# Opening second-order attention inside the second experts' tail: weights, one batch's scales and two tiles made ahead

## The reference

```
logits = einsum('bsh,eh->bse', x, Wg)               # 8 experts, each takes its 128 best tokens of a batch
h1 = gelu(einsum('bekh,ehf->bekf', ex, W1) + b1)     # F = 1024
out = G * (einsum('bekf,efh->bekh', h1, W2) + b2)    # added back to the rows it came from
...
q, k, v = x @ Wq, x @ Wk, x @ Wv                     # 16 heads of 32
S_K = g * S_K + k k';  C_prev = g * C_QV;  G = g * G + k (k' C_prev);  C_QV = C_prev + q v'
o = q' (S_K C_QV - G);   y = o @ Wo                  # g = 0.99, step by step over the tokens
```

## Time and profile before

| what | us |
|---|---|
| median of 3 timed runs | 3533.43 |
| lowest, highest | 3532.81, 3549.98 |
| the profiled execution | 3529.74 |
| its span, first to last instruction | 3527.8 |
| PE busy in it | 3262.7 (92%) |
| DVE, ACT, POOL busy | 2266.3, 2043.5, 1375.0 |

### The profile page before, as it was taken

One profiled execution on the slowest core, in us unless ns is written; L12 is line 12 of the kernel. 1 busy time (PEld: TensorE's weight loads), 2 busy tenths in 40 slices (PEclk: granted clock), 3 DMA queues, 4 the chain that ended last, 5 costly groups with the idle time before them and its releaser, 6 DMA issues. The chain is left out here.

```text
span 3527.8 us, 137586 instructions
## 1 busy us (share of the span) xinstructions
PE 3262.7 (92%) x55606; PEld 2885.2 (82%) x55606; DVE 2266.3 (64%) x6633; ACT 2043.5 (58%) x6370; POOL 1375.0 (39%) x2094
## 2 busy tenths in 40 slices
PE   8938999789965999989999999999998999999998
PEld 7938999777745999978888888888887888888877
DVE  6574555678866555546655555545555788888887
ACT  5555565555535565444444444434443699999996
POOL 5755565300004665423333333333333633333325
PEclk9979999999986999999999999999999999999999
DMA  4144343611134443420000000000001133333333
GB/s 131 49 146 104 89 96 66 169 32 49 56 107 159 95 93 84 105 60 4 4 4 4 4 4 4 4 4 3 4 4 35 31 120 118 118 107 102 104 99 101
DMA packets 202923, 235.34 MB, mean 67 GB/s; under 512 B 17968, under 2 KB 182976, under 8 KB 202304
## 3 DMA queue, kind: packets, MB, share of 16 engines
q1 hardware_dynamic: 177728, 192.99, 17.4%
q0 software_dynamic: 24576, 33.57, 5.6%
HBM read 147.46 MB, written 79.04 MB: 64 GB/s over the span
## 5 line engine op out<-in xcount | busy, mean ns | idle before, releaser
L2518 ACT ACTIVATE wa_S<-wa_S,wa_top 128x192 f32<-128x192 f32 x1024 | 462.7, 475 | 36.6 <-DVE wa_top L2614 36.6
L2057 POOL TENSOR_TENSOR so_OT<-so_O,so_OT 128x128 fp32r<-128x128 f32 x256 | 117.5, 459 | 745.5 <-ACT so_OT L1889 745.5
L1974 DVE TENSOR_TENSOR so_raw<-so_rows,so_masks 128x1024 f32<-128x1024 f32 x256 | 313.4, 1224 | 105.8 <-PE so_rows L1662 98.6
L1968 DVE COPY so_O<-so_bankX 128x128 f32<-128x128 f32 x256 | 74.6, 291 | 416.9 <-PE so_bankX L1775 347.3
L2614 DVE CUSTOM_DVE_ANT_0 wa_S<-wa_bank,wa_band 128x192 f32<-128x192 f32 x1024 | 294.9, 348 | 3.5 <-issue 3.4
L1897 ACT ACTIVATE so_KW<-so_bankU 128x128 f32<-128x128 f32 x256 | 71.2, 278 | 321.1 <-PE so_bankU L1669 321.1
L650 POOL DMA_INDIRECT sum_dram<-y,rows x128 | 223.6, 1747 | 29.4 <-issue 27.2
L2406 PE MATMUL wa_bank<-ident,wa_S 128*128 128x128 f32 x1536 | 221.2, 277 | 7.7 <-ACT wa_probT L2525 4.7
L2518 ACT ACTIVATION_READ_ACCUMULATOR wa_S<-wa_S,wa_top 128x1 f32 x1024 | 222.5, 217 | 0.0
L1691 PE MATMUL so_bankJ<-so_xnT,so_w 128*128 128x256 f32 x1500 | 210.2, 290 | 7.5 <-DVE so_xnT L1948 7.2
L728 ACT ACTIVATE m2e_hT<-m_bank,m2e_bias 128x256 fp32r<-128x256 f32 x256 | 126.9, 496 | 150.2 <-PE m_bank L680 144.2
(11 more groups left out here) (459 smaller groups left out, 9730.9 us busy)
## 6 DMA issues: line engine op xcount, KB each, us to landing
m_w_raw<-in_L_ffn_W_dram SPq DMA_DIRECT2D x64, 512.0 KB, 3.8
wa_V<-wa_V_dram SPq DMA_DIRECT2D x256, 128.0 KB, 3.0
sum_dram<-X SPq DMA_DIRECT2D x16, 1024.0 KB, 4.7
X<-sum_dram SPq DMA_DIRECT2D x16, 1024.0 KB, 8.3
wa_V_dram<-wa_V_new SPq DMA_DIRECT2D x32, 512.0 KB, 3.8
wa_V_rest<-wa_V_dram SPq DMA_DIRECT2D x128, 128.0 KB, 3.3
X<-in_L_attn_a_x_dram SPq DMA_DIRECT2D x8, 1024.0 KB, 11.7
xn_dram<-m2r_xn SPq DMA_DIRECT2D x16, 512.0 KB, 4.5
```

The costliest lines, as they stand in the source:

```text
L1968: nc.vector.tensor_copy(O[:, t % UT], bX[:, O_AT]).then_inc(s_["O_copied"], 1)
L1974: nc.vector.tensor_tensor(AB[:, t % 2].rearrange("p h m t -> p h (m t)"), rows4[:, :, 0:2 * P], masks[:].rearrange("p m t -> p (m t)")[:, ...
L2057: nc.gpsimd.tensor_tensor(OT[:, 1, t % (2 * UT)], O[:, t % UT], OT[:, 0, t % (2 * UT)].bitcast(F32), ALU.subtract).then_inc(s_["O_ready"], 1)
L2518: nc.scalar.activation(S[:, n % 2, z], S[:, n % 2, z], ACT.Exp, bias=top[:, n % 2, z:z + 1], scale=-1.0, accum_out=sums[:, i % 2, SET * c ...
```

## The change

- `w_raw` and the even half of the split weights (`w_even`) are allocated outside the experts' stage and live on. The new class `SecondOrderOpening` lays second-order attention's raw weights into `w_raw` and their high and low parts into `w_even`. The loop's AB and PT go on using the raw weights' place.
- SP: after the last low half of the experts' weights (`w_ready` = 32) it issues the seven weight loads, ahead of the reads of X.
- ACT: after its last gelu, and once expert 6 is through (`down_done` = 28), it casts the four weights, makes the root of batch 0's variances and, instead of POOL, the first two tiles, which go to the place of `R.L`.
- DVE: statistics of batch 0 (8 tiles) ahead of the b2 addition of pair 30; behind its weighing the variances, scales and the low halves of Wq, Wk, Wv, ahead of the b2 addition of pair 31. The statistics of batches 1 to 3 move into steps 2 to 13 of the loop, two a step, their variances into step 14, their scales into step 16.
- PE: the 30 warming products go; the turn of the first tiles stands ahead of the wait for the experts' end. Banks are ordered anew, so that J isn't one that the experts' last product uses.
- SP's masks wait for the last product only (`joined.products`); ACT waits for nothing of `joined`; DVE waits after its low halves.

```diff
--- before.py
+++ after.py
...
+    kept = ExitStack()
+    w_raw = kept.enter_context(nc.sbuf_tensor(f"{tag}_w_raw", [P, QUARTERS, F], F32))
+    w_even = kept.enter_context(nc.sbuf_tensor(f"{tag}_w_even", [P, 2, QUARTERS, F], F32R))
+    if opening:
+        opening.place(kept, w_raw, w_even)
...
+                if opening:
+                    sp.wait_ge(w_ready, PAIRS)
+                    opening.load(sp)
...
+                if opening:
+                    act.wait_ge(down_done, PAIRS - PE_)
+                    opening.cast(act)
+                    opening.root(act)
+                    opening.normalize(act)
...
+                def open_statistics(t, s):
+                    if isinstance(t, int) and t == PAIRS - 1:
+                        dve.wait_ge(R.row_back[0], 16 * (before + 1))
+                        opening.statistics(dve)
+
+                def open_scales(t, s):
+                    if isinstance(t, int) and t == PAIRS - 1:
+                        opening.scales_and_weights(dve)
...
+                if opening:
+                    skewed(dve, PAIRS, [(3, split_xT), (4, split_h), (4, open_statistics), (5, add_b2), (5, weigh), (4, open_scales), (0, split_w)],
+                           unroll=U)
+                else:
+                    skewed(dve, PAIRS, [(3, split_xT), (4, split_h), (5, add_b2), (5, weigh), (0, split_w), (7, stats)], unroll=U)
...
+            joined.products = (down_done, PAIRS)
...
+    def load(self, sp):
+        for n, name in enumerate("qkv"):
+            sp.dma_start(self.w_raw[:, n], self.A[f"L1_attn_a_W{name}"].rearrange("(c p) d -> p c d", p=P)).then_inc(self.sems[f"{name}_loaded"], 16)
+        wo_rows = self.A["L1_attn_a_Wo"].rearrange("(u p) d -> p u d", p=P)
+        for h in range(4):
+            to, of = ((h + 2) % 4 * 32, h * 32)
+            sp.dma_start(self.wo_raw[to:to + 32], wo_rows[of:of + 32]).then_inc(self.sems["o_loaded"], 16)
+
+    def cast(self, act):
+        for n, name in enumerate("qkv"):
+            act.wait_ge(self.sems[f"{name}_loaded"], 16)
+            self.nc.scalar.copy(self.w[:, 0, n], self.w_raw[:, n]).then_inc(self.sems["w_high"], 1)
+        act.wait_ge(self.sems["o_loaded"], 4 * 16)
+        self.nc.scalar.copy(self.wo[:, 0], self.wo_raw).then_inc(self.sems["w_high"], 1)
+
+    def root(self, act):
+        std_of_var(self.nc, act, self.R, self.sems["var_ready"], self.sems["std_ready"], self.FIRST)
+
+    def normalize(self, act):
+        act.wait_ge(self.sems["scaled"], 1)
+        for j in range(2):
+            self.nc.scalar.activation(self.rows[:, j], self.R.X[:, j, :], ACT.Identity, scale=self.R.rstd[:, j:j + 1], bias=self.R.shift[:, j:j + 1]
+                                      ).then_inc(self.sems["rows_ready"], 1)
+
+    def statistics(self, dve):
+        self.chain = Chain(dve, self.sems["step"])
+        for i in range(TB):
+            last = self.nc.vector.bn_stats(self.R.raw[:, i, :], self.R.X[:, i, :])
+        self.chain.then(last)
+
+    def scales_and_weights(self, dve):
+        variances(self.nc, self.chain, self.R, self.sems["var_ready"], self.FIRST)
+        self.low_weights(dve, 0)
+        dve.wait_ge(self.sems["std_ready"], 1)
+        scales(self.nc, self.chain, self.R, self.FIRST)
+        self.nc.vector.memset(self.R.turnstile[:], 0.0).then_inc(self.sems["scaled"], 1)
+        self.low_weights(dve, 1)
+        self.low_weights(dve, 2)
+
+    def low_weights(self, dve, n):
+        dve.wait_ge(self.sems["w_high"], n + 1)
+        self.nc.vector.tensor_tensor(self.w[:, 1, n], self.w_raw[:, n], self.w[:, 0, n].bitcast(F32), ALU.subtract).then_inc(self.sems["w_ready"], 1)
...
-                joined.wait_left(sp)
...
+                sp.wait_ge(*joined.products)
...
-                joined.wait_left(pe)
...
-                for _ in range(30):
-                    nc.tensor.matmul(bC[:, 0:P], R.ident[:], R.ident[:], start=True, stop=True)
                 turn_x(0)
+                joined.wait_left(pe)
...
-                joined.wait_left(act)
-                std_of_var(nc, act, R, s_["var_ready"], s_["std_ready"], FIRST)
...
+                    if t == NEXT_DONE + 1:
+                        std_of_var(nc, act, R, s_["var_ready"], s_["std_ready"], NEXT, 2)
...
-                c = layernorm_scales(nc, dve, R, s_["step"], s_["var_ready"], s_["std_ready"], FIRST)
-                nc.vector.memset(R.turnstile[:], 0.0).then_inc(s_["scaled"], 1)
...
+                joined.wait_left(dve)
...
+                    if NEXT_AT <= t < NEXT_DONE:
+                        for early in range(TB + 2 * (t - NEXT_AT), TB + 2 * (t - NEXT_AT) + 2):
+                            dve.wait_ge(R.row_back[early // TB], 32)
+                            ins = nc.vector.bn_stats(R.raw[:, early, :], R.X[:, early, :])
+                        if t == NEXT_DONE - 1:
+                            c.then(ins)
+                    if t == NEXT_DONE:
+                        variances(nc, c, R, s_["var_ready"], NEXT)
+                    if t == NEXT_DONE + 2:
+                        dve.wait_ge(s_["std_ready"], 2)
+                        scales(nc, c, R, NEXT)
+                        nc.vector.memset(R.turnstile[:], 0.0).then_inc(s_["scaled"], 1)
...
-                normalize(0)
-                normalize(1)
                 pool.wait_ge(s_["w_ready"], 4)
+                pool.wait_ge(s_["QT_ready"], 1)
...
```

More of the change, by code:

```diff
@@ L301, in _, with top_k_experts @@
                     nc.gpsimd.tensor_tensor(R.X[:, i, :], R.X[:, i, :], th[:, i % 4], ALU.add).then_inc(x_ready, 1)
-def top_k_experts(nc, R, tag, A, C, before, with_weights=False):
+def top_k_experts(nc, R, tag, A, C, before, with_weights=False, opening=None):
     E, F, K = 8, 1024, 128
@@ L679, in up @@
                         for n, (c, a, b) in enumerate(steps):
-                            last = nc.tensor.matmul(bank[:, 0:2 * P], w_parts[:, par, a, c, f * P:(f + 1) * P], exT[:, s % 2, b, c],
+                            last = nc.tensor.matmul(bank[:, 0:2 * P], w_parts[par][:, a, c, f * P:(f + 1) * P], exT[:, s % 2, b, c],
                                                     start=(n == 0), stop=(n == len(steps) - 1))
@@ L1541, in _, with __init__, place @@
                     ins.then_inc(XK_ready, 1)
-def second_order_attention(nc, R, A, C, joined):
+class SecondOrderOpening:
+    FIRST = slice(0, TB)
+    def __init__(self, nc, R, A):
+        self.nc, self.R, self.A = nc, R, A
+        self.stage = Stage(nc, "so")
+        names = "step var_ready std_ready scaled rows_ready q_loaded k_loaded v_loaded o_loaded w_high w_ready".split()
+        self.sems = {n: self.stage.sem(n) for n in names}
+        self.rows = R.L[:].rearrange("p i e -> p (i e)").rearrange("p (j d) -> p j d", j=2)
+    def place(self, kept, w_raw, w_even):
+        self.kept = kept
+        raw = w_raw[:].rearrange("p q f -> p (q f)")
+        parts = w_even[:].rearrange("p a q f -> p (a q f)")
+        dense = 3 * HC * 2 * HID
+        self.raw = raw[:, 0:dense]
+        self.w_raw = self.raw.rearrange("p (n c d) -> p n c d", n=3, c=HC)
+        self.wo_raw = raw[:, dense:].rearrange("p (u d) -> p u d", d=HID)
+        self.w = parts[:, 0:2 * dense].rearrange("p (a n c d) -> p a n c d", a=2, n=3, c=HC)
+        self.wo = parts[:, 2 * dense:].rearrange("p (a u d) -> p a u d", a=2, d=HID)
+    def load(self, sp):
[34 more added lines that the diff above has]
+        self.nc.vector.tensor_tensor(self.w[:, 1, n], self.w_raw[:, n], self.w[:, 0, n].bitcast(F32), ALU.subtract).then_inc(self.sems["w_ready"], 1)
@@ L1573, in second_order_attention @@
         rows4 = ps("rows", (P, HG, 512))
-        bU, bC, bX, bJ = (ps(f"bank{n}") for n in "UCXJ")
-        names = """loaded step var_ready std_ready scaled xn_ready xT_done xT_ready QT_done QT_ready KT_done KT_ready V_done V_ready
-                   q_loaded k_loaded v_loaded o_loaded w_high w_ready xT_high O_copied O_high
+        bU, bJ, bC, bX = (ps(f"bank{n}") for n in "UJCX")
+        names = """loaded xn_ready xT_done xT_ready QT_done QT_ready KT_done KT_ready V_done V_ready xT_high O_copied O_high
                    QTg_ready KTg_ready row_done AB_ready PT_ready turned K_ready KQe_ready U_done U_ready Ug_ready C_done WT_ready
@@ L1629, in _ @@
             def _(sp):
-                joined.wait_left(sp)
-                for n, name in enumerate("qkv"):
-                    sp.dma_start(w_raw[:, n], A[f"L1_attn_a_W{name}"].rearrange("(c p) d -> p c d", p=P)).then_inc(s_[f"{name}_loaded"], 16)
-                wo_rows = A["L1_attn_a_Wo"].rearrange("(u p) d -> p u d", p=P)
-                for h in range(HG):
-                    sp.dma_start(wo_raw[crossed_rows(h)], wo_rows[head_rows(h)]).then_inc(s_["o_loaded"], 16)
+                sp.wait_ge(*joined.products)
                 for to, name in ((masks[:, 0], "upper"), (masks[:, 1], "lower"), (decay_t[:], "decay_t"), (to_end[:], "to_end")):
@@ L1678, in turn_x @@
                 def turn_x(p):
```

(17 more changed lines are left out.)

57 lines of the change are left out of this document (26 added, 31 removed).

## The result

The changed kernel takes 3560.02 us (median of 11 runs, 3554.01 to 3567.18), the one before 3540.14 (11 runs beside it, 3529.29 to 3552.80): 1.0053 times as long, 95% interval 1.0037 to 1.0069. The forecast was 3518, with a range of 3513 to 3526 and 0.05 for slower. It is outside the range, on the side of a slower kernel.

The account below looks back on a forecast made before the run. At the seam a chain through DVE, ACT, POOL and the weight loads was taken as the bound, in the loop PE. Terms -17.8 + 0.8 + 1.5 = -15.5 us gave 3514.2 profiled, 3518 as median, range 3513 to 3526.

Parts of the forecast that it names:

- The seam: Between the last expert product and the loop's first rows: rows at 1502.3 instead of 1520.12, gain 17.8 us.
- The b2 addition: DVE's addition for the last pair at the seam: 0.9 us late at most, 0.4 with overlap, taken as 0.8.
- the rule's price: At the seam: if idle PE fell to 1.2 GHz, first projections at half speed, gain 1.3 us smaller; not taken.
- The gather: Experts' second gather before PE's turn of a pair, sharing queues with the early loads: 0.8 us lost, bounds 0 and 6.3.
- The statistics in the loop: Statistics of batches 1 to 3 in steps 2 to 13: 0.6 us lost in step 2, 0.3 in step 3, others hidden.
- The loop. Together 1.5 us lost: The 256-step loop: DVE's moved statistics, variances and scales cost 0.6, 0.3, 0.5 and 0.1 us in steps 2, 3, 14, 16.
- forecast sum: Whole kernel: -17.8 (seam) + 0.8 (gather) + 1.5 (loop) = -15.5 us.
- The slower one: Rival, chance 0.05: without warming products PE's clock falls in the seam's gap and stays down into the first steps, 3539 us.
- Loads hold the gather: Rival, chance 0.10: on the experts' path the early weight loads cost 6.3 us instead of 0.8; gain 10, 3523.5 us.

Follow-up runs that it names:

- e11: The kernel before with 53 filler groups of small PE products, laid to keep block borders off the exposed places of the loop's steps: 3524.62 us, ratio 0.9965.
- e9: The changed kernel with 44 filler groups of small PE products in 23 steps, to keep block borders off the exposed places: 3512.83 us, 0.9936 of the kernel before.
- e5: The changed kernel with 701 filler wait instructions on PE over 26 steps, to keep block borders off the exposed places: 3568.04 us, 1.0097 of the kernel before.
- e12: e10 with the weight loads one pair later still, behind the turn of the last pair (31): 3509.26 us, 0.9899 of the kernel before.
- e7: e5 with second-order attention's weight loads issued later, behind the turn of pair 30: 3565.11 us, 1.0091 of the kernel before.
- e10: e9 with the weight loads issued behind the turn of pair 30, as in e7: 3510.34 us, 0.9927 of the kernel before.
- e4: The changed kernel with 16 one-column PE products (64 instructions) added ahead of the first projection: 3528.69 us, 0.9981 of the kernel before.
- e1: The changed kernel with 30 one-column PE products (120 instructions) added ahead of the first projection: 3541.94 us, 1.0011 of the kernel before.

## Why the prediction was wrong, step by step

**The seam: right.** 17.8 forecast; 18.5 in the profile of the changed kernel, 18.0 between e11 and e9 (27.7 and 9.7 us from the last product's start to the first rows). The b2 addition was 0.8 us less late than taken. The clock stayed at 1.00, as the earlier trace rows had it; in e5 and e12, with the same gap, it didn't, and the first rows came 1.5 us later, about the 1.3 that the prediction gave as the rule's price. So that this term came out at the smaller price is in part luck.

**The gather: right mechanism, too small.** 0.8 forecast, bounds nothing and 6.3. The changed kernel:

```profile
1448.32 1.11 PE L672 MATMUL m_bank<-ident,m4e_ex_in 128*128 128x128 f32 x4 [2.94 <-DMA m4e_ex_in<-xn_dram,rows]
1449.08 6.88 PE L687 MATMUL m_bank<-m4e_exT,m_w_odd 128*128 128x256 f32 x48
```

The second gather goes out at 1442.20, and the turn of its rows starts 6.1 us later instead of 3.0 as in the earlier trace rows. The prediction took the queues as emptying 7 to 9 us after the first load had gone out (1436.33 here). Here they are still full from 1444 to 1446, 8 to 10 us behind it, and the DMA share (the last number but one) falls only then:

```profile
1444.00:1446.00 2.00, 1.38 (x12) 1.18 (x10) 0.58 (x2) 0.00 (x0) 0.00 (x0) 1.00 1.18 276
1446.00:1448.00 2.00, 0.00 (x0) 0.00 (x0) 0.70 (x3) 0.00 (x0) 1.07 (x2) 0.98 0.35 98
```

The stall is 2.94 us, and a second price was not in the sum at all: after it PE ran at half clock.

```profile
1448.30:1450.00 1.70, 1.68 (x8) 1.69 (x9) 0.53 (x1) 0.00 (x0) 1.40 (x2) 0.50 0.45 40
```

The turn took 1.11 instead of 0.60 and the following group 1 us more. Over the stretch it is 4.6 us. e7, e10 and e12 show it to be the loads: later by one pair 1.0 us is left, by two nothing.

**The statistics in the loop: right.** Steps 2, 3 and 14 grew by 0.64, 0.44 and 0.51 us (forecast 0.6, 0.3, 0.5), steps 4 to 13 by less than 0.1. The mask of P in step 2, against the earlier trace rows:

```profile
1509.09 1.23 DVE L2049 TENSOR_TENSOR m_w_raw<-so_rows,so_masks 128x1024 f32<-128x1024 f32 x1 [0.30 <-PE so_rows L1747]
...
1510.89 0.67 DVE L2057 TENSOR_TENSOR m_w_raw<-so_rows,so_masks 128x512 f32<-128x512 f32 x1
1513.40 1.22 DVE L2049 TENSOR_TENSOR m_w_raw<-so_rows,so_masks 128x1024 f32<-128x1024 f32 x1
```

**The step that failed: "The loop. Together 1.5 us lost".** It counted what the change adds to the loop's steps and took the rest of the 256 as unchanged, because no instruction in them changed. The 30 removed products were costed as time and as warmth, not as 120 places in PE's stream. That moved the borders: 51 stalls instead of 12, 45.8 us instead of 10.2. This term of +35.6 turned a gain into a loss. The whole loop lost 42.7, of which 1.6 are the statistics. The rest is there because steps with a stall grow by more than its gap: the steps 45 to 62, 136 to 157 and 235 to 253 of the changed kernel take 53.0 us more than in the kernel before, for 45.8 us of gaps. Why they do wasn't tested. The stalls of the kernel before were to be seen in its trace, as idle time by "issue" in rows that wait for nothing.

**Without it the sum holds.** e9 against e11: gather +4.7, seam -18.0, loop from the first rows to the last mask 1184.8 against 1183.1, +1.8: -11.5. The medians differ by 11.8. The forecast sum was -15.5, and the 4 us between are the gather's 4.7 where 0.8 stood.

**The rivals.** The slower one had the right sign, but its mechanism, a clock that stays down into the first steps, did not happen: the first group of projections ran at full clock. "Loads hold the gather" was nearest to the truth on the experts' side. None had the borders.

## What to carry to other kernels

In an unrolled loop of small products, count the instructions that an edit adds to PE or takes from it ahead of the loop, not only their time. Idle time by "issue" in groups that wait for nothing, at record numbers 256 apart, is a sign that block borders are exposed, and a difference of 1% between two versions can be that alone; compare them with the borders held off the exposed places, as e9 and e11 do. A load moved to an earlier time is to be priced by the late transfer that it meets and by the clock that PE loses while it waits.

## What the hardware showed that I had not expected

- PE seems to run out of instructions. In every stall the first instruction of the new block came 2.1 us or more after the start of the last packet, though these packets took 0.9 to 1.5 us. That it waited for this packet is inferred, not shown by a semaphore or a record.
- The granted clock fell while PE did one-column products, in e4 16 of them behind 1.30 us of idleness: the projections behind them stood at 0.50 of full, 1.2 GHz (window of e4). In e1 each took 0.34 us. Whether the products or the idle time ahead of them let it fall wasn't separated.

```profile
1499.00:1502.00 3.00, 3.00 (x15) 3.00 (x15) 0.00 (x0) 0.19 (x1) 0.00 (x0) 0.50 1.13 292
```

- A wait on a semaphore that has long been passed is not hidden on PE: 701 instructions of two waits each made e5's loop 55.8 us longer than e9's, 0.08 us each, while 704 instructions of small products cost some 0.3 us in each eight steps that hold them (35.2 to 35.5 us).
- The same idle gap of 2.19 us left the clock at full in the changed kernel, e7, e9 and e10, and at half in e5 and e12. What decides this stays open.
- Why only half of the exposed borders stall, in runs of neighbouring steps, stays open too.
